# One fused kernel of a state-space scan and a mixture of experts: rows of B and C by DMA, scan states in PSUM, and late tiles gated on GpSimd

## The reference

```python
# state-space block (256 channels e, 16 states n), z = layernorm(x)
h  = in_proj_w @ ctx.T                            # (256, 256 tokens)
u  = silu(causal_conv4(h) + conv_b)
dt_lo, B, C = split(x_proj_w @ u, [8, 16, 16])
delta = softplus(dt_proj_w @ dt_lo + dt_proj_b)
for t in range(256):
    state = state * exp(delta[:, t, None] * A) + (delta*u)[:, t, None] * B[:, t]
    y[:, t] = state @ C[:, t]
x = x + tanh(g_xattn) * ((y + D * u) * silu(z)).T
# mixture of experts: 2 shared slices and 8 experts, 176 hidden each, top 2
f = layernorm(x)
scores = sigmoid(f @ gate_w.T); w = 2.5 * normalised top-2 of scores
x = x + tanh(g_ffn) * (shared(f) + sum over the top 2 of w * down(silu(gate(f)) * up(f)))
```

## Time and profile before

| | before |
|---|---|
| median of 3 runs | 256.7 us (256.51 to 261.01) |
| profiled execution | 256.38 us |
| its span, first to last instruction | 254.2 us |
| busy: TensorE / VectorE / ScalarE / GpSimd | 218.1 / 215.2 / 175.9 / 186.3 us |
| mean granted TensorE clock | 0.953 |
| DMA | 16.56 MB |

### The profile page before, as it was taken

The page is one execution under the profiler, slowest core; times in us unless marked ns, Lnnn a source line. Parts: engine busy times, 40 slices in busy tenths (PEclk is TensorE's granted clock), DMA queues, the critical chain, the costliest instruction groups (busy, mean ns, idle before and its releaser), DMA issues.

```text
span 254.2 us, 4103 instructions
## 1 busy us (share of the span) xinstructions
PE 218.1 (86%) x1069; PEld 162.8 (64%) x1069; DVE 215.2 (85%) x494; ACT 175.9 (69%) x536; POOL 186.3 (73%) x225
## 2 busy tenths in 40 slices
PE   8960866378787877788999999999999999999995
PEld 3430654154455644456777788788887788888884
DVE  2869999999999999999999999999998698663331
ACT  3489989898889986677767998697765562262230
POOL 0347999999999999999999999988996453220000
PEclk9996599559999999999999999999999999999999
DMA  6369956000700000000160000000000000000000
GB/s 179 123 210 408 380 170 273 1 0 3 331 4 0 0 21 0 1 4 0 44 290 23 1 1 23 0 0 4 22 0 21 0 4 0 21 4 0 8 14 21
DMA packets 7223, 16.56 MB, mean 65 GB/s; under 512 B 888, under 2 KB 6304, under 8 KB 6432
## 3 DMA queue, kind: packets, MB, share of 16 engines
q1 hardware_dynamic: 6912, 16.15, 17.0%
q10 hardware_dynamic: 288, 0.16, 0.2%
HBM read 15.19 MB, written 1.11 MB: 64 GB/s over the span
## 4 chain that ended last, share of the span: by engine, by line
PE 50%; POOL 29%; issue 15%; DVE 3%; ACT 1%; POOLq 0%; DVEq 0%
PE psD L490 14%; PE psU L641 13%; POOL acc L1088 11%; POOL dbu L1048 11%; PE psM L624 4%; PE psU L652 3%; PE psU L653 3%; PE psU L654 3%; PE psC L506 3%; POOL wlo L1109 3%; PE psD L586 1%; POOL dbu L1074 1%; POOL rs L1118 1%; POOL dnc L408 1%; DVE hs L942 1%
## 5 line engine op out<-in xcount | busy, mean ns | idle before, releaser
L1048 POOL TENSOR_TENSOR dbu<-du,bb 128x512 f32<-128x512 f32 x64 | 80.3, 1274 | 6.1 <-DVE du L419 4.3
L678 ACT ACTIVATE psA<-delta,aneg 128x127 f32<-128x127 f32 x256 | 77.7, 358 | 1.5 <-DVE hs L942 1.3
L641 PE MATMUL psU<-wup,hnT 128*128 128x352 f32 x208 | 72.5, 480 | 5.8 <-DVE hcat L856 4.6
L942 DVE TENSOR_TENSOR_SCAN hs<-psA,dbu 128x512 f32<-128x512 f32 x64 | 75.9, 1208 | 0.5 <-POOL dbu L1074 0.2
L1088 POOL TENSOR_TENSOR acc<-acc,prod 128x512 f32<-128x512 f32 x42 | 53.6, 1275 | 8.2 <-DVE prod L951 6.9
L820 ACT ACTIVATE tg<-psU 128x176 f32<-128x176 f32 x80 | 24.8, 314 | 48.7 <-PE psU L641 30.4
L641 PEld LDWEIGHTS psU<-wup,hnT 128*128 128x128 f32 x208 | 38.1, 195 | 24.3 <-DVE hcat L856 7.2
L490 PE MATMUL psD<-wdn,hT 128*128 128x256 f32 x224 | 52.2, 381 | 0.0
L490 PEld LDWEIGHTS psD<-wdn,hT 128*128 128x128 f32 x224 | 41.5, 190 | 5.9
L951 DVE TENSOR_TENSOR prod<-hs,psC 128x512 f32<-128x512 f32 x64 | 41.9, 674 | 1.1 <-POOL acc L1088 1.1
L1022 DVE SCALAR_TENSOR_TENSOR ag<-tg,psU 128x176 f32<-128x176 f32 x80 | 24.6, 327 | 17.7 <-ACT tg L820 17.2
(11 more groups left out here) (117 smaller groups left out, 308.9 us busy)
## 6 DMA issues: line engine op xcount, KB each, us to landing
bb<-brows SPq DMA_DIRECT2D x3, 2048.0 KB, 6.9
wup<-in_w_up SPq DMA_DIRECT2D x2, 1760.0 KB, 11.8
wdn<-in_w_down SPq DMA_DIRECT2D x1, 1664.0 KB, 17.9
x_sb<-in_x SPq DMA_DIRECT2D x4, 256.0 KB, 4.2
bb<-brows SPq DMA_DIRECT2D x1, 1024.0 KB, 4.9
out<-outb SPq DMA_DIRECT2D x8, 128.0 KB, 1.7
bb<-brows SPq DMA_DIRECT2D x1, 512.0 KB, 6.5
ctx_sb<-in_ctxT SPq DMA_DIRECT2D x1, 384.0 KB, 3.9
```

Source lines behind the costliest of these rows:

```text
L641: last = pe.matmul(dst, hnT[:, b % 2, k, lh * P:(lh + 1) * P], wup[:, j, k, :], start=(k == 0), stop=(k == KT - 1))
L678: last = act.activation(dst[:, j, h, 1:], delta[:, b % 2, h, l0 + 1:l1], ACT.Exp, scale=aneg[:, h * DS + s0 + j:h * DS + s0 + j + 1])
L942: dve.tensor_tensor_scan(hs[:, i % 2], psA[:, i % DA_RING], dbu[:, i % DBU_RING], 0.0, ALU.mult, ALU.add).then_inc(s_scan, 1)
L1048: pool.tensor_tensor(tile(dbu[:, m % DBU_RING], m), du[:, b % 2, :, l0:l1].unsqueeze(1).broadcast_to(shape), bb[:, b % 2, s0:s0 + ns, l0:l ...
```

## The change

- B and C both go through `brows`. The rows of C come back by 16 DMAs (`rows_c`), each with the rows for four steps (512 KB) into a ring of three (`cc`). The three-fold x_proj, `parts`, `sel`, the split steps, `spread_b` and `spread_c` are gone.
- `scan` writes its states into PSUM (`psH`, in the banks of psC); `keep_ends` moves from ScalarE to VectorE.
- The router's weights are eight more columns of unit 0, with a tensor of its own (`wup0`); `logits` is gone, `route` works in a strip of psU beside unit 0.
- For tiles 4 to 7 (`FOLD_FROM`) the sum no longer goes to TensorE: GpSimd adds uD (`fold`), the second half (`fold2`) and gates (`gate_y`).
- The first batch is worked in two pieces of 128 tokens; piece 1's projection starts three tokens early (`entry`) and lies in psD, which has double width.
- The weights are fetched by tasks of their own on SP's list, behind `rows_c:2`. The warming matmuls are 6, 11 and 1.
- The lists of all five engines are arranged anew; of SP's the whole is shown, of others the beginning.

```diff
-XROWS = 3 * 2 * DS
+XROWS = 2 * DS
 XM = XROWS + DR
 
-WARM = (6, 20, 1, 6)
-PE_STATES = 8
+WARM = (6, 11, 1)
+CC_RING, CC_STEPS = 3, 4
+CHUNKS = B * DS // CC_STEPS
 DA_RING, DBU_RING, PROD_RING, HT_RING = 2, 3, 3, 4
...
+PIECES = B + 1
+
+
+def piece(p):
+
+    return (0, p * P, (p + 1) * P) if p < LH else (p - 1, 0, L)
+
+
+def pieces_for(m):
+
+    return 1 if m < HALF else m // DS + 2
+
+
+FOLD_FROM = 4
...
     "SyncE": """
-        xproj:0 dt:0 xproj:1 dt:1 xproj:2 dt:2 finish:0 xproj:3 dt:3 finish:1 finish:2 finish:3 finish:4
-        finish:5 finish:6 finish:7
+        xproj:0 dt:0 rows_c:0 rows_c:1 xproj:1 dt:1 rows_c:2 fetch:0 fetch:1 fetch:2 rows_c:3 xproj:2 dt:2
+        rows_c:4 rows_c:5 rows_c:6 xproj:3 dt:3 rows_c:7 rows_c:8 finish:0 rows_c:9 rows_c:10 rows_c:11 xproj:4
+        dt:4 finish:1 rows_c:12 rows_c:13 finish:2 rows_c:14 rows_c:15 finish:3 finish:4 finish:5 finish:6
+        finish:7
...
-        z_stats:0 z_stats:1 z_stats:2 z_stats:3 first:0 scan:0 scan:1 scan:2 scan:3 scan:4 weights_lo:0 scan:5
...
+        z_stats:0 z_stats:1 first:0 scan:0 scan:1 z_stats:2 z_stats:3 scan:2 scan:3 scan:4 scan:5 scan:6 scan:7
+        carry:0 weights_lo:0 scan:8 fix:8 fix:9 carry:1 scan:9 fix:10 scan:10 scan:11 fix:11 fix:12 weights_lo:1
+        variance:0 scan:12 prod:9 delta0:2 fix:13 prod:10 scan:13 scan:14 fix:14 fix:15 prod:11 delta1:2 prod:12
+        delta2:2 prod:13 scan:15 scan:16 scan:17 scan:18 prod:14 scan:19 prod:15 prod:17 scan:20 prod:18 scan:21
...
-        load:0 z_stats:0 tap0:0 tap1:0 tap2:0 silu_u:0 z_stats:1 z_stats:2 z_stats:3 split0:0 split1:0 split2:0
-        log_1:0 log_2:0 delta0:0 delta1:0 tap0:1 delta2:0 tap1:1 tap2:1 scan:0 scan:1 prod:0 silu_u:1 scan:2
-        prod:1 prod:2 scan:3 scan:4 prod:3 split0:1 scan:5 prod:4 prod:5 scan:6 scan:7 split1:1 z_gate:0
-        split2:1 prod:6 prod:7 scan:8 scan:9 gate_y:0 prod:8 prod:9 residual:0 log_1:1 stats:0 scan:10 scan:11
...
+        load:0 tap0:0 tap1:0 tap2:0 silu_u:0 tap0:1 tap1:1 tap2:1 z_stats:0 silu_u:1 z_stats:1 log_1:0 z_stats:2
+        z_stats:3 log_2:0 delta0:0 delta1:0 log_1:1 delta2:0 log_2:1 delta0:1 scan:0 scan:1 delta1:1 keep_ends:0
+        keep_ends:1 tap0:2 prod:0 prod:1 tap1:2 tap2:2 scan:2 scan:3 prod:2 prod:3 keep_ends:2 keep_ends:3
+        silu_u:2 scan:4 delta2:1 scan:5 z_gate:0 keep_ends:4 keep_ends:5 prod:4 prod:5 scan:6 scan:7 prod:6
...
-        hs = sb("hs", [P, 2, W])
+        cc = sb("cc", [P, CC_RING, CC_STEPS * NS, P])
...
-        psC = ps("psC", [P, 2, 512])
+        psH = ps("psH", [P, 2, W])
         psM = ps("psM", [P, 512])
         psU = ps("psU", [P, 2, 512])
-        psD = ps("psD", [P, D])
-        psB = psD[:, :].rearrange("p (k l) -> p k l", k=EH)
+        psD = ps("psD", [P, 2 * D])
+        psB = psD[:, 0:D].rearrange("p (k l) -> p k l", k=EH)
...
+        def entry(p):
+
+            b, l0, l1 = piece(p)
+            lo = l0 - DC + 1 if p == 1 else l0
+            view = (psD if p == 1 else psM)[:, :].rearrange("p (h l) -> p h l", h=EH)
+            return view[:, :, 0:l1 - lo], lo
...
+        def strip(k):
+
+            return psU[:, 0, 2 * FF + k * NE:2 * FF + (k + 1) * NE]
...
                 if task == "xproj":
+                    b, l0, l1 = piece(i)
                     sp.wait_ge(s_xd, i + 1)
-                    sp.dma_start(brows[i], xdbl[0:DS, :]).then_inc(d_brow, 16)
+                    sp.dma_start(brows[b, :, l0:l1], xdbl[0:XROWS, l0:l1]).then_inc(d_brow, 16)
                 elif task == "dt":
+                    b, l0, l1 = piece(i)
                     sp.wait_ge(d_brow, 16 * (i + 1))
+                    if b >= 2:
+                        sp.wait_ge(s_dbu, DS * (b - 1))
+                    n0 = 0 if i else 2 * NS
                     if i == 0:
-
-                        for n0, n1, l0 in ((PE_STATES, DS, 0), (0, PE_STATES, P)):
-                            sp.dma_start(bb[:, 0, n0:n1, l0:L], brows[0, n0:n1, l0:L].unsqueeze(0).broadcast_to(
-                                [P, n1 - n0, L - l0])).then_inc(d_bb, 16)
-                        sp.dma_start(wg[:, :, :], w_gate).then_inc(d_wg, 16)
-                        for k in range(2):
-                            sp.dma_start(wup[:, NU // 2 * k:NU // 2 * (k + 1)],
-                                         w_up[:, NU // 2 * k:NU // 2 * (k + 1)]).then_inc(d_wup[k], 16)
-                        sp.dma_start(wdn[:, 0:FB - 1, :],
-                                     w_down[0:(FB - 1) * P].rearrange("(f p) d -> p f d", p=P)).then_inc(d_wdn, 16)
-                        sp.dma_start(wdn[0:LASTF, FB - 1, :], w_down[(FB - 1) * P:FCAT]).then_inc(d_wdn, 16)
-                    else:
-                        if i >= 2:
-                            sp.wait_ge(s_dbu, DS * (i - 1))
-                        sp.dma_start(bb[:, i % 2], brows[i].unsqueeze(0).broadcast_to([P, DS, L])).then_inc(d_bb, 16)
+                        sp.dma_start(bb[:, 0, 0:n0, l0:l1], brows[0, 0:n0, l0:l1].unsqueeze(0).broadcast_to(
+                            [P, n0, l1 - l0])).then_inc(d_first, 16)
+                    sp.dma_start(bb[:, b % 2, n0:DS, l0:l1], brows[b, n0:DS, l0:l1].unsqueeze(0).broadcast_to(
+                        [P, DS - n0, l1 - l0])).then_inc(d_bb[i], 16)
+                elif task == "rows_c":
+                    b, s0, ns, l0, l1 = step_range(CC_STEPS * i)
+                    sp.wait_ge(d_brow, 16 * pieces_for(CC_STEPS * i))
+                    if i >= CC_RING:
+                        sp.wait_ge(s_prod, CC_STEPS * (i - CC_RING + 1))
+                    n = CC_STEPS * NS
+                    sp.dma_start(cc[:, i % CC_RING], brows[b, DS + s0:DS + s0 + n, l0:l1].unsqueeze(0).broadcast_to(
+                        [P, n, P])).then_inc(d_cc[i % CC_RING], 16)
+                elif task == "fetch" and i == 0:
+                    sp.dma_start(wup0[:, :, :], w_up0).then_inc(d_wg, 16)
+                    sp.dma_start(wup[:, 0:NU // 2 - 1], w_up[:, 0:NU // 2 - 1]).then_inc(d_wup[0], 16)
+                elif task == "fetch" and i == 1:
+                    sp.dma_start(wup[:, NU // 2 - 1:], w_up[:, NU // 2 - 1:]).then_inc(d_wup[1], 16)
+                elif task == "fetch":
+                    sp.dma_start(wdn[:, 0:FB - 1, :],
+                                 w_down[0:(FB - 1) * P].rearrange("(f p) d -> p f d", p=P)).then_inc(d_wdn, 16)
+                    sp.dma_start(wdn[0:LASTF, FB - 1, :], w_down[(FB - 1) * P:FCAT]).then_inc(d_wdn, 16)
...
-                    if unit == 0 or unit == NU // 2:
+                    if unit == 0:
+                        pe.wait_ge(d_wg, 16)
+                    if unit == 1 or unit == NU // 2:
                         pe.wait_ge(d_wup[unit // (NU // 2)], 16)
                     if j == 0:
                         pe.wait_ge(s_hnT, t + 1)
                     if unit >= 2:
                         pe.wait_ge(s_mul, unit - 1)
-                    else:
-                        pe.wait_ge(s_bb, unit + 1)
                     dst = psU[:, unit % 2, 0:2 * FF]
-                    if j not in SLOT or t < SPLIT[SLOT[j]][1]:
+                    if j == 0:
+                        dst = psU[:, unit % 2, 0:2 * FF + NE]
                         for k in range(KT):
-                            last = pe.matmul(dst, hnT[:, b % 2, k, lh * P:(lh + 1) * P], wup[:, j, k, :],
+                            last = pe.matmul(dst, hnT[:, b % 2, k, lh * P:(lh + 1) * P], wup0[:, k, :],
+                                             start=(k == 0), stop=(k == KT - 1))
+                    elif j not in SLOT or t < SPLIT[SLOT[j]][1]:
...
-                    act.activation(psM[:, :], xh[:, :, :].rearrange("p h l -> p (h l)"), ACT.Tanh).then_inc(s_tu, 1)
-                    if i == 0:
+                    b, l0, l1 = piece(i)
+                    act.activation(split(dense(i)), xh[:, :, l0:l1], ACT.Tanh).then_inc(s_tu, 1)
+                    if i == 1:
                         act.preload_act_table_set("natural_log_exp_and_others")
...
-                    act.wait_ge(s_log, i + 1)
-                    act.activation(psB[:, 0, 0:NE], psB[:, 0, 0:NE], ACT.Exp, scale=-1.0).then_inc(s_rex, 1)
+                    act.wait_ge(s_up, NU * i + 1)
+                    act.activation(strip(0), strip(0), ACT.Exp, scale=-1.0).then_inc(s_rex, 1)
...
+                elif task == "keep_ends":
+                    b = i // DS
+                    dve.wait_ge(s_scan, i + 1)
+                    if b >= 1:
+                        dve.wait_ge(s_carry, 2 * b)
+                    dve.tensor_copy(ends[:, i % HALF, :], psH[:, i % 2].rearrange("p (c l) -> p c l", l=P)[:, :, P - 1]
+                                    ).then_inc(s_ends, 1)
                 elif task == "scan":
                     b, s0, ns, l0, l1 = step_range(i)
                     dve.wait_ge(s_dA, i + 1)
...
                         dve.wait_ge(s_ends, ends_of(i - 2))
                     if second_half(i):
                         dve.wait_ge(s_fix, ends_of(i))
```

(49 more changed lines are left out.)

418 lines of the change are left out of this document (183 added, 235 removed).

## The result

The changed kernel takes 253.01 us (median of 4 runs, 252.58 to 253.55), the kernel before 256.51 us in the same comparison: ratio 0.987, 95% interval 0.984 to 0.990. That is 3.5 us or 1.3% less, within the 2% that I called no change; the forecast was 247.5 us and 3.5%. Its profiled execution is 253.55 us with a span of 251.7 us and a mean granted clock of 0.919 (before: 0.953); it is the longest of the four, 0.5 us over their median.

What follows compares the result with a forecast made beforehand. Scans on VectorE and GpSimd set the pace to 134 us, all three engines are full to 190, then TensorE alone. 256.4 - 9.5 (TensorE) - 0.4 (start) + 1.6 (new idle) - 0.6 (VectorE) = 247.5 us; range 240 to 256.

Steps and rivals of the forecast that it cites:

- the 4.8 us: VectorE work that would have to slip behind 190 us; a third, 1.6 us, taken as new TensorE idle time.
- Rival (a): VectorE and GpSimd bind everywhere; TensorE's gain shrinks to about 4 us, the folds cost 2: 254 us, chance 0.20.
- spreads: TensorE behind 134 us: 12 sets of matmuls spreading C go, 2.7 us saved.
- logits: TensorE behind 134 us: separate router matmuls of five tiles become columns of unit 0, 1.7 us saved, 0.1 us added.
- start: First product near 17 us, first scan near 18.3: -4.0 us, of which -0.4 us counts after work moved behind it.
- keep_ends over the splits: VectorE's full stretch: 32 copies moved from ScalarE add 4.8 us; three split steps of batches 1 to 3 save 3.7.
- three two-SBUF-input steps: VectorE's delta0:1, delta1:1 and delta2:1 at the start, beside a busy GpSimd: +0.3 us charged, bounds 0 and 3.6.
- 43 ns of bounds: VectorE's scans writing PSUM stay at 1.21 us, within -43 to +43 ns each; taken at zero over 60 scans.
- rival (d): VectorE pays for PSUM after all, 0.12 us on each scan and prod: +14 us, 262 us, chance 0.05.
- rival (c): TensorE's clock falls to 1.2 GHz for two 20 us stretches ahead of 134 us: 267 us, chance 0.06.
- the 70 us that I had named as a sign of being wrong: In the profile after, a granted TensorE clock under 1 behind 70 us would show the forecast wrong.
- "route waits for tanh of unit 0, which is long done": Among the other edits: the route's wait for unit 0's tanh, long done; no time was charged.

Runs made afterwards that it cites:

- a_late: Changed kernel with the third matmul of each split unit left out in tiles 6 and 7 only (3.3 us of TensorE): 251.89 us, ratio to before 0.977.
- a_early: Changed kernel with the third matmul of each split unit left out in tiles 2 to 5 only (5.8 us of TensorE): 252.62 us, ratio to before 0.980.
- a_warm2: Changed kernel with 15 extra warming matmuls of zeros, three ahead of each task from prod:0 to prod:3: 253.78 us, ratio to before 0.987.
- a_hs: Changed kernel with the scan states in SBUF again in place of PSUM: 285.83 us, ratio to before 1.111.
- a_route: Changed kernel with the route working in SBUF, behind the second unit's mul: 276.97 us, ratio to before 1.077.
- a_p: Changed kernel with GpSimd's additions into acc made for 110 of each 128 tokens, 8 us off GpSimd: 250.87 us, ratio to before 0.976.

## Why the prediction was wrong

Its direction was right, its size was two and a half times what came (8.9 us forecast against the profiled execution, 3.5 measured by the medians). Step by step:

**The step that failed** is "So one microsecond less of TensorE work is worth one microsecond only behind 134 us, and only if VectorE and GpSimd can deliver tiles earlier", and with it the term "I take a third of the 4.8 us as new TensorE idle time, 1.6 us". The condition was not met. Behind 134 us TensorE gained 4.3 us of idle time, nearly the upper bound of 4.8, and its busy time fell by 2.8 us less than the sum had it, 1.6 of them work taken over from ahead of 134 us, where I had taken nothing for the change: 7.1 us given back in place of 1.6, which is 5.5 of the 6.1 us between 247.5 us and the profiled execution. The cuts show the same by another way: 9.0 us of TensorE time were worth 1.4 us after and 2.6 us before, and a_late and a_early put most of that behind about 205 us. In the kernel before the rows that made TensorE look like the bound (55.8 of 56.0 us) were true but not sufficient: VectorE at 54.3 and GpSimd at 53.0 had 1.7 and 3.0 us to give.

**Rival (a)** comes nearest, 254 us at 0.20. It was right that VectorE and GpSimd bind until 190 us and that only the shorter tail pays: the last scan came 0.7 us later than before, the last features 3.2 us sooner behind it. It was wrong to make the folds cost 2 us: their undoing makes the kernel slower. And cutting VectorE and GpSimd together gave 5.8 us for 16 us of work, far more than the two cuts apart but a third of the work, so these two are not the whole bound either.

**The terms.** The removed work on TensorE is gone as counted (no L559 group). The folding was put at 5.2 us of TensorE and 1.7 of VectorE; less new idle time that was 4 to 5 us, and it is worth 4.4. Since the whole is 3.5 us, spreads, logits, start and the rest together cost 0.9 us where the sum had a gain: 4.3 us for spreads and logits, 0.4 for the start, less 1.1 for keep_ends over the splits. That is where the forecast's size was lost; which of them pays nothing no run tells.

**The start** was right, though the steps listed add up to -4.2 us and not to the -4.0 written: first product 17.23 us (near 17), first scan 18.71 (18.3), and the gain used up by the moved work by the fifth scan. One of the three two-SBUF-input steps met GpSimd (0.99 us), which costs 0.57 against the 0.3 I charged. The rows of B and C were hidden, the weights but for ScalarE's 1.5 us.

**VectorE's prices:** scan 1218 ns for 1208, product 679 for 674, within the 43 ns of bounds; rival (d) is out. keep_ends take 4.1 us for 32, where I took 4.8; one takes 150 ns, as I had it, but two side by side overlap. The Trainium skill (VectorE: DVE Perf Modes, the section on the TRN2 errata) gave an estimated 129 ns each and 4.1 us by its fixed part for PSUM sources; the group L941 has that total, but with 150 ns each. **GpSimd's prices:** 0.73 us for each 256-column operation, not half of 1.27; 2.2 us per tile and not 1.9. The trace of the kernel before had this price, in `hnlo` (L1104, 128x256, 732 ns), and I halved a wider operation instead.

**The clock, rival (c):** it fell as feared in kind, not in place. The three stages of 20 us were at 0.74, 0.66 and 1.00; 20 to 40 us is at 0.63 now, and the last low stretch, 69.0 to 75.5 us, at 0.76: just past the 70 us that I had named as a sign of being wrong. Later stages are at 0.99 to 1.00, and a_warm2 shows that the low level from 20 to 40 us costs nothing measurable.

**The lock.** In a_hs VectorE's products with two SBUF inputs cost 0.37 us more on the mean of 64 beside GpSimd, and 32 of them took over 0.8 us, which none does with the states in PSUM. That fits the rule in the section "SBUF: two separate sides" of the Trainium skill (SBUF - State Buffer), which I had charged at 0.3 us and bounded at 3.6. The same section of the Trainium skill names a second kind, single-input operations in a two-port mode. The small ones that were held (the 128x8 tensor_scalar, the four-column copy) fit it; the reciprocals were not held. That these used such a mode no run shows. The changed kernel avoids it for its products by its choice of PSUM for the states; two of its four z_gates, two inputs in SBUF, still took 0.88 and 1.12 us in place of 0.67 to 0.70.

**Left open:** what the merged logits are worth, and why TensorE idles 2.7 us more ahead of 134 us. One candidate is that bank 0 of psU is held until the route has run: TensorE's wait for the product of unit 0 (L865) is 3.8 us from 20 to 134 us, 1.1 us before (L852). "route waits for tanh of unit 0, which is long done" priced the wait of VectorE and not what is queued behind the bank. That is argued from waits, and no run here tells it apart. The exact coupling of the orders was not traced either, ScalarE's among them; the cuts show that VectorE and GpSimd are tied, and by how much.

## What to carry to other kernels

When two or three engines are each over 95% busy in the same stretch under hand-written orders, a microsecond taken from one of them was worth nothing to a third of one here, and one taken from the two fullest together (16 us for 5.8) a third, while a microsecond of delay put on the path was worth a whole one (3.4 us arrived as 3.3, 33.7 us of VectorE time as 32.8). Before pricing a saving at its full size, cut that much work from the engine in the kernel before and time it: one run of that sort (9.0 us gave 2.6) speaks against counting 9.5 us nearly whole. Look also for edits that take a cross-engine wait out of the fullest in-order queue: the folding, the one part shown to pay here, did so for the last two tiles, though how much of its gain that was is open.

## What the runs showed of the hardware

In a_route a VectorE operation from SBUF to SBUF with eight columns took up to 2.21 us beside GpSimd's products (median of eight 0.54), 13 times the 167 ns that it takes on PSUM, while reciprocals on the same tile took 0.15 to 0.20 us. In a_hs a product of 512 columns went from 679 to a mean of 1054 ns, with a longest of 2158, by having both inputs in SBUF, and a four-column copy from a median of 150 to 162 ns with a longest of 1246. GpSimd's operations of 256 columns took 0.73 us, those of 440 columns 1.13 (a_p) and those of 512 columns 1.28 to 1.30 us: by these an estimated fixed part of 0.16 to 0.2 us and 2.2 ns per column.
